# A decoder layer with experts: norm rows turned by DMA instead of TensorE, score weights folded, weight pairs converted in the shared blocks

## What is computed

```
q, k, v = split(norm(x) @ W);  q = elu(q) + 1;  k = elu(k) + 1
x = x + (q @ (k^T v)) / (q @ sum(k) + eps)                    # linear attention
q = norm(x) @ Wq + bq;  k = ctx @ Wk + bk;  v = ctx @ Wv + bv
x = x + softmax(q k^T / 16) @ v                               # cross attention
y = norm(x)
x = x + gelu(y @ Wfc_s + b) @ Wproj_s + b                     # shared block
      + sum over the best 2 of 8 experts e of gate_e * (gelu(y @ Wfc[e] + b) @ Wproj[e] + b)
```

## Time and profile before

| | |
|---|---|
| runs | median 899.22 us of 3 (898.44 to 900.22) |
| profiled execution | 902.8 us, span 901.0 us, mean granted clock 0.977 |
| TensorE busy | 846.3 us, 94% |
| VectorE busy | 635.8 us, 71% |
| ScalarE busy | 391.7 us, 43% |
| GpSimd busy | 266.5 us, 30% |
| a pair of splits in the blocks (L945, L946), mean | 300 and 428 ns |
| stage loads, 512 KB, median to landing | 4.6 and 5.6 us |

### The profile page before, as it was taken

How to read it: one execution, slowest core, us unless ns; L and a number is a source line. 1 busy time by engine, 2 the same in 40 slices (tenths; PEclk the granted TensorE clock), 3 DMA queues, 4 the chain that set the end, 5 groups by cost and what they waited for, 6 DMA issues and landing times.

```text
span 901.0 us, 23891 instructions
## 1 busy us (share of the span) xinstructions
PE 846.3 (94%) x7011; PEld 721.9 (80%) x7012; DVE 635.8 (71%) x1937; ACT 391.7 (43%) x817; POOL 266.5 (30%) x234
## 2 busy tenths in 40 slices
PE   3899999999987999999989999999999999999995
PEld 1677777777875887899978888888888888888884
DVE  4769898989866868766656666666666666666663
ACT  4466665757533455444433333333333333333331
POOL 2221222222211077750001333333333333333333
PEclk9999999999975999999999999999999999999998
DMA  5544646453200177541142433323343433333430
GB/s 185 169 126 126 191 126 180 148 150 116 77 28 30 37 244 232 194 135 58 58 84 54 62 57 59 63 50 59 56 64 58 66 62 59 57 60 59 61 54 7
DMA packets 116804, 84.72 MB, mean 94 GB/s; under 512 B 59132, under 2 KB 112152, under 8 KB 116760
## 3 DMA queue, kind: packets, MB, share of 16 engines
q1 hardware_dynamic: 102456, 67.06, 27.8%
q0 software_dynamic: 14304, 17.10, 11.1%
HBM read 37.84 MB, written 37.88 MB: 84 GB/s over the span
## 4 chain that ended last, share of the span: by engine, by line
PE 67%; issue 11%; DVE 7%; DMA 6%; ACT 4%; POOL 3%; SPq 1%; DVEq 0%; POOLq 0%; ACTq 0%
PE bank L1133 10%; PE bank L1135 10%; PE bank L1134 10%; PE bank_kv L1147 5%; PE bank_kv L1148 5%; PE bank_kv L1149 5%; PE bank_st L1147 5%; PE bank_st L1149 5%; PE bank_st L1148 5%; DMA stage_w<-in_L_ffn_Wfc 3%; POOL w_parts L504 1%; DVE w_parts L711 1%; POOL rstd L513 1%; DMA stage_w<-in_L_ffn_Wproj 1%; PE bank L994 1%
## 5 line engine op out<-in xcount | busy, mean ns | idle before, releaser
L677 ACT ACTIVATE expert_buffers<-bank,bias_columns 128x256 f32<-128x256 f32 x440 | 208.3, 474 | 362.8 <-PE bank L1135 273.0
L1133 PE MATMUL bank<-expert_buffers,w_parts 128*128 128x256 f16 x880 | 241.6, 275 | 10.9 <-ACT expert_buffers L677 8.5
L945 DVE TENSOR_SCALAR expert_buffers<-expert_buffers 128x256 f16<-128x256 f32 x440 | 131.8, 300 | 156.9 <-ACT expert_buffers L677 114.7
L1135 PE MATMUL bank<-expert_buffers,w_parts 128*128 128x256 f16 x880 | 241.5, 274 | 0.0
L1134 PE MATMUL bank<-expert_buffers,w_parts 128*128 128x256 f16 x880 | 241.5, 274 | 0.0
L946 DVE SCALAR_TENSOR_TENSOR expert_buffers<-expert_buffers 128x256 f16<-128x256 f32 x440 | 188.3, 428 | 15.2
L556 POOL DMA_INDIRECT out<-expert_buffers,token x78 | 121.8, 1562 | 20.9 <-issue 20.8
L1147 PE MATMUL bank_kv<-w_parts,expert_buffers 128*128 (+1 forms) x448 | 122.7, 274 | 0.5 <-DVE expert_buffers L946 0.2
L1148 PE MATMUL bank_kv<-w_parts,expert_buffers 128*128 (+1 forms) x448 | 122.6, 274 | 0.0
L1149 PE MATMUL bank_kv<-w_parts,expert_buffers 128*128 (+1 forms) x448 | 122.5, 274 | 0.0
L1147 PE MATMUL bank_st<-w_parts,expert_buffers 128*128 (+1 forms) x432 | 118.1, 273 | 0.3 <-DVE expert_buffers L946 0.3
(11 more groups left out here) (142 smaller groups left out, 1239.4 us busy)
## 6 DMA issues: line engine op xcount, KB each, us to landing
rows_by_expert<-expert_buffers SPq DMA_DIRECT2D x13, 795.0 KB, 7.8
stage_w<-in_L_ffn_Wfc SPq DMA_DIRECT2D x16, 512.0 KB, 4.6
stage_w<-in_L_ffn_Wproj SPq DMA_DIRECT2D x16, 512.0 KB, 5.6
expert_buffers<-in_L_ffn_bproj SPq DMA_DIRECT2D x39, 128.0 KB
rows<-in_x SPq DMA_DIRECT2D x16, 256.0 KB, 7.3
x_residual<-rows SPq DMA_DIRECT2D x16, 256.0 KB, 2.2
expert_buffers<-x_residual SPq DMA_DIRECT2D x16, 256.0 KB, 2.8
out<-expert_buffers SPq DMA_DIRECT2D x16, 256.0 KB, 3.7
```

Source lines behind the costliest of these rows:

```text
L677: act.activation(g32[f % 2], hid[f % 2][:, 0:BLK], ACT.Gelu_apprx_tanh, bias=bias, scale=UNSCALE).then_inc(s["gelu_done"], 1)
L945: chain(dve.tensor_scalar(g[:, 0, :], g32[f % 2], A_SCALE, None, ALU.mult), "g_hi", c + 1)
L1133: pe.matmul(hid[f % 2][:, 0:BLK], w_hi, x[:, 0, k, :], start=k == 0, stop=False)
L1135: op = pe.matmul(hid[f % 2][:, 0:BLK], w_lo, x[:, 0, k, :], start=False, stop=k == DK - 1)
```

## The change

- The rows of all three norms are turned by DMA. ScalarE writes the high part of the normalized rows (`high`), VectorE the low part (`low`), both before the turning and from SBUF; SyncE issues a DMA transpose from SBUF to SBUF for each norm (`turn_norm`, and for the third norm one for each of its two tiles of 128 rows).
- The third norm's turned rows of all sequences are kept (`store`, in the room of the weights), and the shared blocks read them from there. `transpose_rows` and its copies are gone. The logits are made from pairs.
- Wq and Wk are folded once, at steps 0 and 1 (`transpose_weight`, `fold_weights`), so that the second norm's rows are multiplied with the folded keys and the projection with Wq is gone; a row and two columns carry the biases. The scores are made of fp16 pairs.
- Only the shared weights' two halves are converted in the attention stage. The sixteen halves of the experts are converted one a shared block. The routing's sixteen parts lie in four blocks, four in each.
- A result's two tiles lie in one PSUM bank (`ysum`), and a hidden tile in each bank of `bank_st`.
- The shared blocks are written out, and the first two routed blocks' rows are fetched without a wait for the blocks before.

```diff
+        store = w2[:, 8 * 2048:16 * 2048].rearrange("p (b t l k n) -> p b t l k n", b=B, t=TB, l=2, k=DK)
+        regions = [[words(w1, 12, 4), 0, 4096], [words(w1, 4, 4), 0, 4096], [words(w2, 4, 4), 0, 4096],
+                   [words(w2, 0, 4), 0, 4096], [words(w1, 0, 4), 0, 4096]]
...
+        hid = [bank_st[:, c, :] for c in range(2)]
+        ysum = [bank_kv[:, c, :].rearrange("p (t n) -> p t n", t=TB) for c in range(2)]
...
+            def turn_norm(n, b):
+                got(sp, f"lo{n + 1}_ready", b)
+                got_if(sp, "q_done" if n == 0 else "scores_done", b - 1)
+                sp.dma_start_transpose(xnT[n].rearrange("p t l k n -> p (t l k) n"),
+                                       halves16[n].rearrange("p t l n -> p (t l n)")).then_inc(s[f"turned{n + 1}"], 16)
...
+                if live(i - 2):
+                    turn_norm(1, i - 2)
+                if live(i - 4):
+                    b = i - 4
+                    got(sp, "lo3_ready", b)
+                    got_if(sp, "logits_done", b - 1)
+                    for t in range(TB):
+                        sp.dma_start_transpose(store[:, ds(b, 1), t].rearrange("p b l k n -> p (b l k) n"),
+                                               rows16[:, ds(b * TB + t, 1), 0:2 * D].rearrange("p a n -> p (a n)"))\
+                            .then_inc(s["turned3"], 16)
+                if live(i + 1):
+                    turn_norm(0, i + 1)
...
-            for G in range(CONVERT_FROM):
+            for G in range(NSH - 1):
+                load_half(G, G + 2)
                 shared_block(G, G % 2)
-            sp.wait_ge(s["routed"], 1)
-            for q in range(LAST):
-                load_half(2 * E - LAST + q, HALVES - LAST + q)
-                shared_block(CONVERT_FROM + q, (CONVERT_FROM + q) % 2)
-            with sp.Fori((CONVERT_FROM + LAST - 1) // 2, NSH // 2 - 1) as j:
-                for c in range(2):
-                    shared_block(2 * j + (1 + c), (1 + c) % 2)
+            load_half(NSH - 1, NSH + 1)
             sp.wait_ge(s["rows_sent"], 2 * TILES * 16)
...
+                if not (isinstance(n, int) and n < 2):
+                    sp.wait_ge(s["up_done"], FC * (n + (NSH - 1)))
...
+            def high(n, b):
+                got(act, f"xn{n + 1}_ready", b)
+                if not (isinstance(b, int) and b == 0):
+                    act.wait_ge(s[f"turned{n + 1}"], 16 * b)
+                act.activation(halves16[n][:, :, 0, :], xn[n], ACT.Copy, scale=A_SCALE).then_inc(s[f"hi{n + 1}_ready"], 1)
...
+                if live(i - 4):
+                    b = i - 4
+                    got(act, "xn3_ready", b)
+                    act.wait_ge(s["x2_stored"], (b + 1) * 16)
+                    act.activation(rows16[:, ds(b * TB, TB), 0:D], xn[2], ACT.Copy, scale=A_SCALE)\
+                        .then_inc(s["hi3_ready"], 1)
...
-                    if isinstance(G, int) and 0 <= G - CONVERT_FROM < LAST:
-                        half = 2 * E - LAST + G - CONVERT_FROM
-                        if f == 1:
-                            convert_last(half, w1, stage1[:, :], "w1_loaded", "w1_hi")
-                        elif f == 3:
-                            convert_last(half, w2, flat_stage[1], "w2_loaded", "w2_hi")
+                    if isinstance(G, int) and G < NSH:
+                        if f == 2:
+                            convert_last(G, w1, stage1[:, :], "w1_loaded", "w1_hi")
+                        elif f == 4:
+                            convert_last(G, w2, flat_stage[1], "w2_loaded", "w2_hi")
...
+            def low(n, b):
+                got(dve, f"hi{n + 1}_ready", b)
+                dve.scalar_tensor_tensor(halves16[n][:, :, 1, :], xn[n], A_SCALE, halves16[n][:, :, 0, :],
+                                         ALU.mult, ALU.subtract).then_inc(s[f"lo{n + 1}_ready"], 1)
...
+                if live(i - 2):
+                    low(1, i - 2)
...
-                    dve.wait_ge(s["x2_stored"], (b + 1) * 16)
-                    got(dve, "xn3_ready", b)
-                    hi = rows16[:, ds(b * TB, TB), 0:D]
-                    lo = rows16[:, ds(b * TB, TB), D:2 * D]
-                    chain(dve.tensor_scalar(hi, xn[2], A_SCALE, None, ALU.mult), "hi_step", b + 1)
-                    dve.scalar_tensor_tensor(lo, xn[2], A_SCALE, hi, ALU.mult, ALU.subtract).then_inc(s["xf_ready"], 1)
+                    got(dve, "hi3_ready", b)
+                    dve.scalar_tensor_tensor(rows16[:, ds(b * TB, TB), D:2 * D], xn[2], A_SCALE,
+                                             rows16[:, ds(b * TB, TB), 0:D], ALU.mult, ALU.subtract)\
+                        .then_inc(s["lo3_ready"], 1)
...
+                    for m in range(DK):
+                        dve.scalar_tensor_tensor(key16[:, m, 1, :], k2T_ps[:, m, :], key_bias[:, m:m + 1],
+                                                 key16[:, m, 0, :], ALU.add, ALU.subtract)
+                    dve.scalar_tensor_tensor(row16[0:1, 1, :], row_ps[0:1, :], row_bias[0:1, :], row16[0:1, 0, :],
+                                             ALU.add, ALU.subtract).then_inc(s["key_ready"], 1)
...
-                    if isinstance(G, int) and G < 2:
-                        route(FC * G + f)
+                    if isinstance(G, int) and G < 4 and f < 4:
+                        route(4 * G + f)
                     if f == 2 and not (isinstance(G, int) and G == 0):
                         evacuate(G - 1, 1 - parity, shared=before == "shared", prior=(G - 1) // 2 if isinstance(G, int) else prior)
-                    if isinstance(G, int) and 0 <= G - CONVERT_FROM < LAST:
-                        half = 2 * E - LAST + G - CONVERT_FROM
+                    if isinstance(G, int) and G < NSH:
                         if f in (4, 5):
-                            split_last(half, w1, stage1[:, :], "w1_hi", "w1_lo", f - 4)
-                        elif f in (6, 7):
-                            split_last(half, w2, flat_stage[1], "w2_hi", "w2_lo", f - 6)
+                            split_last(G, w1, stage1[:, :], "w1_hi", "w1_lo", f - 4)
+                        elif f == 7 or (f == 6 and G < NSH - 1):
+                            for chunk in (0, 1) if G == NSH - 1 else (f - 6,):
+                                split_last(G, w2, flat_stage[1], "w2_hi", "w2_lo", chunk)
...
+            def fold_weights():
+                pe.wait_ge(s["wkT_copied"], 1)
+                pe.wait_ge(s["wqT_copied"], 1)
                 for m in range(DK):
                     for k in range(DK):
+                        op = pe.matmul(fold_ps[:, m, :], wkT[:, k, tile(m)], wqT[:, k, :], start=k == 0, stop=k == DK - 1)
+                op.then_inc(s["fold_done"], 1)
+                pe.wait_ge(s["bias_ready"], 1)
+                for col, w, bias in ((0, wqT, bk), (DK, wkT, bq)):
+                    for m in range(DK):
+                        for k in range(DK):
+                            pe.matmul(cols_ps[:, col + m:col + m + 1], w[:, k, tile(m)], bias[:, k:k + 1],
+                                      start=k == 0, stop=k == DK - 1)
+                for k in range(DK):
+                    op = pe.matmul(cols_ps[0:1, 2 * DK:2 * DK + 1], bq[:, k:k + 1], bk[:, k:k + 1],
+                                   start=k == 0, stop=k == DK - 1)
+                op.then_inc(s["cols_done"], 1)
...
+                    pe.wait_ge(s["turned2"], 16 * (b + 1))
+                    got(pe, "key_ready", b)
                     got(pe, "v2_ready", b)
+                    if isinstance(b, int) and b == 0:
+                        pe.wait_ge(s["sixteen_set"], 1)
                     for t in range(TB):
-                        for m in range(DK):
-                            op = pe.matmul(sc_ps[:, t, :], q2T[:, m, tile(t)], k2T[:, m, :], start=m == 0, stop=m == DK - 1)
+                        for l in range(2):
+                            pe.matmul(sc_ps[:, t, :], sixteen[0:1, :], row16[0:1, l, :], start=l == 0, stop=False)
+                        for k in range(DK):
+                            for a, c in PASSES:
+                                op = pe.matmul(sc_ps[:, t, :], xnT[1][:, t, a, k, :], key16[:, k, c, :],
+                                               start=False, stop=(k, a, c) == (DK - 1, 1, 0))
                     op.then_inc(s["scores_done"], 1)
...
+                    pe.wait_ge(s["turned3"], 16 * TB * (b + 1))
                     if isinstance(b, int) and b == 0:
+                        pe.wait_ge(s["wr_ready"], 1)
+                    got_if(pe, "logits_copied", b - 1)
                     for t in range(TB):
                         for k in range(DK):
+                            for a, c in PASSES:
+                                op = pe.matmul(lg_ps[:, t, :],
+                                               store[:, ds(b, 1), t, a, k, :].rearrange("p b n -> p (b n)"),
+                                               wr16[:, k, c, :], start=(k, a, c) == (0, 0, 0),
```

(38 more changed lines are left out.)

311 lines of the change are left out of this document (130 added, 181 removed).

## The result

Before 899.7 us, after **932.7 us** (medians of four runs each, 932.3 to 933.7 after). The ratio is 1.038 with an interval of 1.034 to 1.041. The forecast was 887, and its range ended at 918. The profiled execution took 932.6 us with a span of 930.5.

What follows compares the result with a forecast made beforehand. TensorE and VectorE were taken to fill the attention step, a TensorE-SyncE loop to set it afterwards. 902.8 less 1.0 (attention stage) less 11.0 (shared blocks) gave 890.8, as a median 887 us; range 866 to 918.

Steps and rivals of the forecast that it cites:

- the loop's sum of 15.1 us: Attention steps: TensorE and SyncE cycle through ctx load and transposes, 14.6 to 15.8 us, taken as 15.1 against 15.57 before.
- the clock as a rival: Attention steps: TensorE's clock falls in every step behind its wait, 21 to 60 us lost, total 915; chance 0.17.
- The sign that the prediction had named: Attention steps: a granted clock below 0.9 would make the prediction wrong; 1.00 was expected from 60 to 240 us.
- The sizes inside the loop: Attention-step cycle: 5.3 us from ctx load to landed pair, logits 0.7, TensorE's work from logits to L1078's end 9.8.
- Steps 14 to 18: Late attention stage: the first two steps gain nothing, the later ones lose their transposes; -0.6 us.
- Start: Start of the attention stage: folding the weights adds TensorE work and two waits; +2.5 us, between -2 and +6.
- VectorE's part: Attention steps: VectorE's loop falls from 15.57 to 13.8 us, with L788 at 0.16 to 0.2.
- the rival gave VectorE: Attention steps: VectorE's loop binds, steps at 13.8 to 14.0 us instead of 15.1, total 873; chance 0.19.
- that rival was wrong: SyncE's queue: transposes out of SBUF hold it longer, at twice 1.24 us for 256 KB total 922; chance 0.13.
- Shared blocks: Shared blocks: transposes and conversion stalls go (-8.6 us), the first routed block's wait goes (-2.4); sum -11.0.
- the 1.0 that I took: Shared blocks: 1.0 us in all for sixteen converting blocks whose stage loads come 0.3 us late.

Runs made afterwards that it cites:

- experiment 2: Changed kernel plus ten, or five, unread 128x512 matmuls ahead of TensorE's wait for the third norm's turned rows: 914.2 us with ten, 917.0 with five.
- experiment 3: Changed kernel with the third norm's transposes issued ahead of the second's: 908.7 us; or with the second norm's transpose split into two of 128 KB: 954.1 us.
- experiment 4: Changed kernel with the third norm's transposes ahead of the second's and five unread matmuls in TensorE's remaining wait: 965.3 us beside 974.8 before, ratio 0.990.
- experiment 6: Changed kernel, ctx load last, ScalarE's high part and first routed rows earlier; plus late-step unread matmuls: 868.0 us, last logits' too: 941.9 (ratio 0.966), search moved too: 949.5.
- one more move: On the changed kernel with ctx load last: ScalarE's third-norm high part ahead of the exponentials; run also had first routed rows turned earlier: 872.0 us, ratio 0.966.
- first kernel of experiment 6: Unread matmuls in TensorE's waits from step 16, added to the kernel with ctx load last, ScalarE's high part and first routed rows earlier: 868.0 us, ratio 0.964.

## Why the prediction was wrong

**The step that failed: the loop's sum of 15.1 us, taken at full clock.** The prediction named the loop, its wait (2 to 3 us before L1143: 2.61) and the clock as a rival. It kept the rival out of the sum and at a chance of 0.17, with one row against it in which 1.90 us of standing left the state fast. Here a wait of 1.17 us was followed by half clock, one of 1.5 us in every second step (experiments 2 and 3). A row in which the clock survives bounds nothing. The sign that the prediction had named, a clock below 0.9 in the steps, came in six of the ten stretches of 20 us from 80 to 280. The clock's share is 1.9 us a step (experiment 2), a third more than the 1.4 read off L1047 alone.

**The sizes inside the loop, +1.3 us a step.** SyncE's stretch from the ctx load to the turned pair is 5.8 (125.41 to 131.22) where I took 5.3, between 4.8 and 6.0. A small transpose's hold was at the upper end (1.26), its landing at the lower (2.5), and about 0.1 passes between two issues. The logits were 0.7 and are 1.6 (131.22 to 132.79): 1.06 for twelve narrow matmuls and a gap of 0.51. Everything behind them fits: experiment 2 has 10.6 from the logits to the end of L1110, 9.0 without them, and the forecast had 9.8 and 9.1. With one issue out and the wait filled, the step came to 14.91 (experiment 4).

**Steps 14 to 18, +11.0 against -0.6.** I carried the same loop into the first two, so its error came along: 35.7 us instead of 28.9. In the other three TensorE has little work and the clock stays low; filling the waits gave 7.3 us back on a kernel with the same tail (experiment 6).

**Start +4.6 against +2.5.** Inside its range of -2 to +6. TensorE's first L1072 started at 15.14, 1.2 later than the earlier trace rows, and the two fold groups take 1.9 each.

**VectorE's part held.** L788 takes 0.17 where it took 1.42. Once the loop through SyncE is gone, the step is 14.16 and with one more move 13.59, beside the 13.8 that the rival gave VectorE; 873 for that rival, 879 and 872 measured. But filling VectorE's gap did not shorten that step (experiment 6), so the nearness to 13.8 is in part luck.

**The transposes out of SBUF** hold SyncE 1.24 to 1.26 us for 256 KB, as out of DRAM; that rival was wrong.

**Shared blocks, -7.1 against -11.0.** Sixteen converting blocks cost TensorE 1.1 us of waiting for gelu, as the 1.0 that I took, and 0.8 for VectorE's splits. Missing was the first routed block: its rows were turned at 493.90, behind three transfers that wait for block 14 to be evacuated, and landed 6.6 us later, where the median of these transposes is 3.2. The prediction took the free buffer for the only condition and did not look at what stood ahead in the queue. With the rows turned earlier, the blocks take 172.7 to 173.7 us (176.0 in the first kernel of experiment 6), and the forecast was 173.8.

## What to carry to other kernels

Where a load in an in-order queue waits for the step's own result, everything behind it is in a loop with the engine that produces it: put it last. Price a wait on TensorE not by its length but with the work behind it at half clock, and let one row of the opposite only lower the chance, not the price. Unread matmuls in a wait tell the clock's part from the wait's in one run, and were worth 18 us here, though they did not keep the clock up in every step.

## What the runs showed of the hardware

- **More matmuls, less time.** Ten unread matmuls a step, 2.3 us of TensorE work, took 18 us off the kernel.
- **A transpose's hold on the queue does not go by its size.** In the full steps of the changed kernel 1.24 to 1.28 us for 128 KB and for 256 KB; among other transfers single ones held it up to 2.3; the landing goes by size, 2.5 and 3.2 us.
- **The same twelve narrow matmuls take 0.45 or 1.06 us at full clock.** The twelve matmuls of L1143 take 1.06 to 1.09 us in the looped steps and 0.51 more pass before L1047, also at granted clock 1.00. In step 4, which is written out, they take 0.46 behind a wait of 2.36 us, without a gap, and in the looped steps of the kernels that don't wait 0.45. The difference is 1.1 us a step. It is not that TensorE had stood: in experiment 4 the unread matmuls run until 0.1 us before (last two rows), and the twelve still take 1.08. No run here writes the loop out, and the cause is open:

```profile
77.27 0.46 PE L1143 MATMUL bank<-w_parts 128*128 128x8 f16 x12 [2.36 <-DMA w_parts<-rows]
77.72 3.66 PE L1047 MATMUL bank_st<-w_parts 128*128 128x257 f32 x8
...
94.17 1.09 PE L1143 MATMUL bank<-w_parts 128*128 128x8 f16 x12 [2.56 <-DMA w_parts<-rows]
95.77 3.79 PE L1047 MATMUL bank_st<-w_parts 128*128 128x257 f32 x8 [0.52 <-issue]
...
103.15 1.24 PE L1138 MATMUL bank_kv<-w_parts 128*128 128x512 f16 x5
104.54 1.08 PE L1146 MATMUL bank<-w_parts 128*128 128x8 f16 x12
```

- **Two chips lose 75 us while rows are scattered.** There the kernel before takes 975 us. In the kernels of experiment 6 that were traced there, ScalarE's L701 waits 77 to 80 us in four to six pieces, up to 30.8, for something outside the profile (45 us in the kernel of experiment 4). The stages ahead take the same time as elsewhere (stage ends 260.7 and 261.0 beside 261.3). The cause is open; each total is compared with the kernel before on the same chip.
